# Second step of a forward 2-D transform: from fp32 matmuls to three fp16 passes over a split operand

## The chip, the cores and the metric

The kernel runs on one core of a Trainium2 chip. The metric is the device time of one execution in microseconds, the median of several runs. TensorE multiplies (its results land in PSUM), ScalarE and VectorE read PSUM and write SBUF, GpSimd is a third elementwise engine, and SyncE issues the DMAs. Each engine works through its own instructions in order, and the engines wait for each other through semaphores.

## The reference, cut to what matters

The input is `x` of shape (8, 128, 128, 128): 8 images, 128 channels, 128 x 128 pixels, fp32. The first of two layers takes the two-dimensional Fourier transform of every channel of the group-normalised image:

```
xf = jnp.fft.fft2(x)                       # x: b, c, h, w
qf = xf.reshape(b, HEADS, hd, h * w)       # frequency attention uses qf
g  = sigmoid(conv(relu(bn(conv(xf.real, w1)))))
out_f_l = jnp.abs(jnp.fft.ifft2(g * xf))
```

Everything after it (attention over heads, gates, inverse transform, spatial attention from 3x3 and 5x5 convolutions, and a second layer with a state-space scan) is left as it is by the change.

## The kernel before, in words

`layer0` does layer 0 in a hardware loop over the 8 images, `layer1` does layer 1 after it. Within an image the stages follow each other: load and group normalisation, **forward transform**, a Gram matrix over the spectrum, gates, inverse transform, head mixing, and the convolutions. This document is about the forward transform.

The forward transform of an image is done in `NK` = 32 steps of 4 channels (line 520). Step `t` has these parts, and each engine has them in its own program order:

- TensorE, `stage1(t)` (lines 1095 to 1100): 4 matmuls, each with one channel (128 x 128, fp32, from `xh`) as the stationary operand and the 128-column table `fwd` (65 cosine and 63 sine columns) as the moving one. They fill the PSUM bank `bk[t % 2]`.
- ScalarE, lines 1386 to 1389: one copy of 128 x 512 from that bank to `AB[:, t % 2]` in SBUF, two buffers in turn. Semaphore `s_ab` counts these copies.
- TensorE, `stage2(t)` (lines 1102 to 1111): 4 matmuls with a 128 x 128 cosine or sine table as the stationary operand and the 4 x 65 cosine part or the 4 x 63 sine part of `AB` as the moving one, two that accumulate in bank `bk[2 + t % 2]` (real part) and two in `bk[4 + t % 2]` (imaginary part). Each fp32 matmul shows as two records in the trace.
- ScalarE, `xr_copy(t)` (1380 to 1384) and VectorE, `xi_copy(t)` (712 to 716): each moves its part of the spectrum from PSUM to `XR`, `XI` (128 x 256) and `XLAST` (128 x 4) in SBUF.

The orders are these. TensorE: stage1(0), then for each t stage1(t+1), stage2(t). `stage1(t)` waits until the copy of step t-2 has left its bank; `stage2(t)` waits for the copy of step t and for both spectrum copies of step t-2. ScalarE: copy(t), xr_copy(t-1), and in steps 4, 12, 20 and 28 in addition `normalise` (1376 to 1378), which normalises a quarter of the image in place (128 x 4096). VectorE:

```
columns(0)
columns(1)
for i in range(8):
    for t in range(4 * i, 4 * i + 4):
        xi_copy(t)
    if i + 2 < 8:
        columns(i + 2)
```

`columns(i)` (718 to 722) normalises the 16 channels of group i in `xh` (two instructions over 128 x 2048), which the four `stage1` of that group read. `xh` has two buffers. The load of group i+2 is issued by SyncE (1008 to 1013) once `stage1(4i+3)`, the last reader of the buffer, is done: the kernel waits at line 1010 and then issues two DMAs of 8 channels.

Matmuls of all these stages are recorded under line 1066, ScalarE's operations under line 1365, since small helpers (`mm`, `cp`) issue them.

Of the kernel before, what the change touches and what calls it, by code (L numbers as in the profile page):

```python
# [27 lines left out]
F16 = mybir.dt.float16  # L28
ALU = mybir.AluOpType
# [12 lines left out]
NP = 6  # L42
T3W, T5W = 3 * NP, 5 * NP
VROWS = (0, 64, 1, 64, 64, 64, 64, 126, 64, 127)
XSCALE, WMAX = 32.0, 16384.0


# [82 lines left out]
def layer0(nc, B, x, table, shift_d, w, wts, y_d, of_d, x1, gn2):  # L130
# [3 lines left out]
    with ctx:  # L134
# [4 lines left out]
        def count(name, per):  # L139
            counters.append(Count(sem(name), per))  # L140
            return counters[-1]
# [51 lines left out]

        wk = lambda o, n: work[:, o:o + n]
        xh = wk(0, 4096).rearrange("p (s c w) -> p s c w", s=2, w=P)
        AB = wk(4096, 1024).rearrange("p (s c u) -> p s c u", s=2, u=P)
        T8 = wk(5120, 1024).rearrange("p (w j) -> p w j", j=JG)
        gates = wk(0, UG * P).rearrange("p (u c) -> p u c", c=P)
        Z = wk(2048, 2048).rearrange("p (s c n) -> p s c n", s=2, c=4)
# [173 lines left out]
        def _(dve):  # L373
# [8 lines left out]
            def link(op):  # L382
                s_ch[0] += 1
                op.then_inc(s_link, 1)
                dve.wait_ge(s_link, s_ch[0])
# [4 lines left out]
            for n, (name, _) in enumerate(plan):  # L390
                dve.wait_ge(s_ld, ld_at[n])
                if name == "first":
                    g = lambda i: par8[0:8, i:i + 1]
                    link(nc.vector.tensor_scalar(g(5), g(4), 1e-5, None, ALU.add))
                    dve.wait_ge(s_sq, 1)
                    link(nc.vector.reciprocal(g(5), g(5)))
                    link(nc.vector.tensor_tensor(g(6), g(1), g(5), ALU.mult))
                    link(nc.vector.tensor_tensor(g(7), g(0), g(3), ALU.subtract))
                    link(nc.vector.tensor_tensor(g(7), g(7), g(6), ALU.mult))
                    did(nc.vector.tensor_tensor(g(7), g(7), g(2), ALU.add))  # L400
                    dve.wait_ge(s_pe, next(npe))
                    nc.vector.tensor_copy(gate_sb[:, :], bk[0][0:UG * JG, 0:2])
                    nc.vector.tensor_copy(temps[:, :], bk[1][:, 0:2])
                    nc.vector.tensor_copy(w1t[:, :], bk[2][:, 0:8])
                    for i in range(4):
                        m = min(4, UG - 4 * i)
                        link(nc.vector.tensor_copy(gate_w[:, 4 * i:4 * i + m, :], bk[3 + i][0:UG * JG + 1, 0:m * P]))
                    link(nc.vector.tensor_copy(valid[:, :, :], ks["valid"].rearrange("t (r n) -> t r n", n=P)))
                    link(nc.vector.tensor_copy(vfix[:, :, :], ks["vfix"].rearrange("t (r n) -> t r n", n=P)))
                    link(nc.vector.memset(relu_r[:, :, :], 1.0))  # L410
                    did(nc.vector.memset(B8[:, :, :], 0.0))
                    nc.vector.memset(norms[:, 0, 0:1], 0.0).then_inc(s_go, 1)
                elif name.startswith("proj"):
                    dve.wait_ge(s_pe, next(npe))
                    s = int(name[4:])
                    link(nc.vector.tensor_copy(pt[:, 2 * s, :], bk[0][:, 0:P]))
                    did(nc.vector.tensor_copy(pt[:, 2 * s + 1, :], bk[1][:, 0:P]))
                    nc.vector.memset(norms[:, 0, 1:2], 0.0).then_inc(s_go, 1)
                elif name.startswith("qk"):
                    _, off, size = name.split()  # L420
                    off = int(off)
                    link(nc.vector.tensor_tensor(btap, ks["tap"].rearrange("p (t s) -> p t s", s=T5), bcol.unsqueeze(1).broadcast_to([P, T5, T5]), ALU.mult))
                    did(nc.vector.tensor_tensor(sparse, ks["mpair"].unsqueeze(1).broadcast_to([P, T5, 64]), w5.unsqueeze(2).broadcast_to([P, T5, 64]), ALU.mult))
                    dve.wait_ge(s_pe, next(npe))
                    dst = WBt if size == "5" else WAfull
                    for i in range(4):
                        m = min(8, T5 - 8 * i)
                        link(nc.vector.tensor_copy(dst[:, 8 * i:8 * i + m, off:off + 64], bk[i][:, 0:m * 64].rearrange("p (t o) -> p t o", o=64)))
                    did(nc.vector.tensor_copy(bias_sum[:, int(size == "5"), off:off + 64], bk[4][0:T5, 0:64]))
                    dve.wait_ge(s_ve, done[0])  # L430
                    nc.vector.memset(w5, 0.0).then_inc(s_go, 1)
                else:
                    s = int(name[3:])
                    for i in range(2):
                        dst = (WVt, WCt)[s].rearrange("p t (g i) -> p t g i", i=2)[:, :, :, i]
                        link(nc.vector.tensor_tensor(dst, ks["mgroup"].unsqueeze(1).broadcast_to([P, T5, 64]), w2[:, i, :].unsqueeze(2).broadcast_to([P, T5, 64]), ALU.mult))
                    if s == 0:
                        link(nc.vector.tensor_tensor(vtap[:, :, :], ks["vt"].rearrange("p (t s) -> p t s", s=T5), bcol.unsqueeze(1).broadcast_to([P, T5W, T5]), ALU.mult))
                    nc.vector.memset(w2, 0.0).then_inc(s_go, 1)
# [95 lines left out]
        s_xn = count("s_x_normalised", 4)  # L535
        s_xhn = count("s_columns_normalised", 8)
        s_s1 = count("s_stage1", NK)
        s_ab = count("s_stage1_copied", NK)
        s_s2 = count("s_stage2", NK)
        s_xr = count("s_real_copied", NK)  # L540
        s_xi = count("s_imag_copied", NK)
# [104 lines left out]

        @block.vector
        def _(dve):
            credit(dve, v, s_shi, s_xhn, s_xi, s_h1c, s_gx, vq, vf, s_pq, s_lq, s_pf, s_lf, s_ud, s_y, s_fd, s_ms, s_bvc, s_oa, s_x1, s_bn)
            V = nc.vector  # L650

            n0 = [0]
# [4 lines left out]
            with dve.Fori(0, B) as b:  # L657
# [54 lines left out]
                def xi_copy(t):  # L712
                    dve.wait_ge(s_s2.sem, s_s2.at(b, t + 1))
                    spectrum = bk[4 + t % 2][:, 0:4 * HALF].rearrange("p (c u) -> p c u", u=HALF)
                    V.tensor_copy(XLAST[:, 1, 4 * t:4 * t + 4], spectrum[:, :, U64])
                    V.tensor_copy(XI[:, 4 * t:4 * t + 4, :], spectrum[:, :, 0:U64]).then_inc(s_xi.sem, 1)

                def columns(i):
                    dve.wait_ge(sxh[i % 2], b * 128 + 32 * (i // 2) + 32)
# [2 lines left out]
                    V.tensor_tensor(t_, t_, rows[:, P + 16 * i:P + 16 * i + 16].unsqueeze(2).broadcast_to([P, 16, P]), ALU.add).then_inc(s_xhn.sem, 1)  # L722

                columns(0)
                columns(1)
                for i in range(8):
                    for t in range(4 * i, 4 * i + 4):
                        xi_copy(t)
                    if i + 2 < 8:
                        columns(i + 2)  # L730
# [333 lines left out]
        def _(pe):  # L1064
# [15 lines left out]
            with pe.Fori(0, B) as b:  # L1080
# [13 lines left out]

                def stage1(t):
                    pe.wait_ge(s_xhn.sem, s_xhn.at(b, t // 4 + 1))
                    pe.wait_ge(s_ab.sem, s_ab.at(b, t - 1))
                    for c in range(4):
                        m = mm(bk[t % 2][:, c * P:(c + 1) * P], xh[:, t // 4 % 2, 4 * (t % 4) + c, :], k["fwd"], start=True, stop=True)
                    m.then_inc(s_s1.sem, 1)  # L1100

                def stage2(t):
                    pe.wait_ge(s_ab.sem, s_ab.at(b, t + 1))
                    pe.wait_ge(s_xr.sem, s_xr.at(b, t - 1))
                    pe.wait_ge(s_xi.sem, s_xi.at(b, t - 1))
                    A, Bm = AB[:, t % 2, :, 0:HALF], AB[:, t % 2, :, HALF:]
                    for o, (ca, cb_) in ((bk[2 + t % 2], (k["cs"][:, 0:P], k["cs"][:, P:])), (bk[4 + t % 2], (k["sc"][:, 0:P], k["cs"][:, 0:P]))):
                        o3 = o[:, 0:4 * HALF].rearrange("p (c u) -> p c u", u=HALF)
                        mm(o3, ca, A, start=True, stop=False)
                        m = mm(o3[:, :, 1:64], cb_, Bm, start=False, stop=True)  # L1110
                    m.then_inc(s_s2.sem, 1)

                stage1(0)
# [249 lines left out]
        def _(act):  # L1363
            credit(act, a, s_row, s_hq, s_hf, s_last, s_sq, s_tt, s_trc, s_shr, s_xn, s_ab, s_xr, s_t8c, s_rel, s_sig, s_z, s_abs, s_uc, s_mc, s_os, s_of)
            cp = lambda o, i, f=ACT.Copy, **kw: nc.scalar.activation(o, i, f, **kw)  # L1365
            with act.Fori(0, B) as b:
# [13 lines left out]
                def xr_copy(t):  # L1380
                    act.wait_ge(s_s2.sem, s_s2.at(b, t + 1))
                    spectrum = bk[2 + t % 2][:, 0:4 * HALF].rearrange("p (c u) -> p c u", u=HALF)
                    cp(XLAST[:, 0, 4 * t:4 * t + 4], spectrum[:, :, U64])
                    cp(XR[:, 4 * t:4 * t + 4, :], spectrum[:, :, 0:U64]).then_inc(s_xr.sem, 1)

                for t in range(NK):
                    act.wait_ge(s_s1.sem, s_s1.at(b, t + 1))
                    act.wait_ge(s_s2.sem, s_s2.at(b, t - 1))
                    cp(AB[:, t % 2, :, :].rearrange("p c u -> p (c u)"), bk[t % 2][:, :]).then_inc(s_ab.sem, 1)
                    if t > 0:  # L1390
                        xr_copy(t - 1)
                    if t % 8 == 4:
                        normalise(t // 8)
# [839 lines left out]
```

## Time and profile before

| | us |
|---|---|
| median of 3 runs | 26842.19 |
| lowest and highest | 26841.0, 26844.8 |
| the profiled execution, its own time | 26840.82 |
| span of the profiled execution, first to last instruction | 26839.0 |
| TensorE busy in the span | 23909.5 |
| VectorE busy | 19661.7 |
| ScalarE busy | 13616.0 |
| GpSimd busy | 12340.1 |

Read the busy times as averages over stages that have different limits: about half of the span is layer 0 and half is layer 1. The forward transform of one image takes about 100 us of an image's 1,640 us in layer 0. Times in the rows are microseconds from the span's start, unless ns is written.

### The profile page before, as it was taken

What the parts mean: (1) busy time and instruction counts of PE and PEld (TensorE: products, weight loads), DVE (VectorE), ACT (ScalarE), POOL (GpSimd) and SP (SyncE); (2) the same over time, 40 slices, a digit from 0 to 9 for tenths busy, and PEclk for the clock granted to TensorE, in tenths of its full rate; (3) what the DMA queues carried; (4) which work ended last, traced back from release to release, by engine and by line L of the source; (5) the groups of instructions that cost most, each with busy time, mean ns of one, the idle gap of its engine ahead of it and who ended that gap; (6) DMA issues with size and microseconds to landing.
All of it is one profiled execution on the core that took longest, in us unless ns stands there. A gap on an engine that the chain in (4) does not pass through costs nothing. (4 is left out here: it accounts for less than half of the span.)

```text
span 26839.0 us, 328765 instructions
## 1 busy us (share of the span) xinstructions
PE 23909.5 (89%) x108001; PEld 14269.1 (53%) x108001; DVE 19661.7 (73%) x22753; ACT 13616.0 (51%) x19703; POOL 12340.1 (46%) x4613
## 2 busy tenths in 40 slices
PE   6988989889898998989988888888888888888888
PEld 4776867768677676877733333333333333333333
DVE  3562635537255372644699999999999999999999
ACT  1413223131321413214277777777777777777777
POOL 0000000000000000000099999999999999999998
PEclk7998989989898998989999999999999999999999
DMA  1121121211202112021244444444444444444444
GB/s 53 49 76 61 33 65 38 76 61 42 66 32 73 61 55 69 27 66 57 75 178 165 193 165 173 183 167 191 169 169 185 169 191 166 167 189 167 190 168 163
DMA packets 816277, 3112.23 MB, mean 116 GB/s; under 512 B 61865, under 2 KB 325434, under 8 KB 530362
## 3 DMA queue, kind: packets, MB, share of 16 engines
q1 hardware_dynamic: 815802, 3106.12, 31.1%
q8 instruction: 271, 4.44, 0.1%
q14 instruction: 204, 1.67, 0.0%
HBM read 2813.61 MB, written 292.30 MB: 116 GB/s over the span
## 5 line engine op out<-in xcount | busy, mean ns | idle before, releaser
L2176 POOL TENSOR_TENSOR hid<-hid,bc 128x2048 f32<-128x2048 f32 x2048 | 7814.6, 3816 | 909.2 <-DVE carry L2082 906.5
L1845 PE MATMUL yp<-hid,ident 128*128 128x512 f32 x16384 | 7344.7, 597 | 430.7 <-POOL hid L2176 430.7
L2150 POOL TENSOR_SCALAR_AFFINE_SELECT ident<-ident 128x128 f32<-128x128 f32 x1 | 0.3, 294 | 13331.3 <-DVE ident L2035 13331.3
L1845 PEld LDWEIGHTS yp<-hid,ident 128*128 128x128 f32 x16384 | 3039.7, 189 | 4628.3 <-issue 3957.9
L2068 DVE TENSOR_TENSOR_SCAN hid<-da,carry,t 128x512 f32<-128x512 f32 x3968 | 4857.8, 1266 | 111.0 <-DVE carry L2082 7.7
L2074 DVE TENSOR_TENSOR_SCAN hid<-t,carry,hid 128x512 f32<-128x512 f32 x3968 | 4828.1, 1258 | 29.2 <-ACT t L1916 28.5
L2169 POOL TENSOR_TENSOR hid<-bc,du 128x1024 f32<-128x1024 f32 x2048 | 4101.4, 2003 | 197.0 <-PE yp L1845 170.6
L1066 PE MATMUL bk<-region 128*128 128x256 f16 (+2 forms) x32688 | 3946.9, 279 | 24.6 <-ACT region L1365 19.1
L1066 PEld LDWEIGHTS bk<-region 128*128 128x128 f16 (+2 forms) x32688 | 3400.0, 119 | 603.9 <-issue 175.8
L1916 ACT ACTIVATE t<-delta,v_a 128x512 f32<-128x512 f32 x4096 | 2660.0, 681 | 1574.0 <-DVE hid L2074 1570.9
L1801 PE MATMUL pj<-xn,w_x 128*128 128x512 f32 x4096 | 2376.5, 734 | 1079.2 <-ACT xn L1941 1031.0
L1066 PE MATMUL bk<-work,region 128*128 128x256 f16 x27336 | 3151.6, 273 | 23.9 <-DVE region L960 20.3
L1066 PEld LDWEIGHTS bk<-work,region 128*128 128x128 f16 x27336 | 2643.9, 99 | 498.6 <-issue 74.5
L1927 ACT ACTIVATE t<-bc 128x1024 f32<-128x1024 f32 x2048 | 2096.6, 1024 | 1437.7 <-DVE hid L2068 1387.1
L1904 ACT ACTIVATE da<-delta,v_a 128x512 f32<-128x512 f32 x4096 | 2703.2, 707 | 0.3 <-DVE delta L2110 0.3
L2054 DVE TENSOR_TENSOR t<-t,du 128x1024 f32<-128x1024 f32 x2048 | 2479.0, 1210 | 256.4 <-ACT t L1927 256.2
L1365 ACT ACTIVATE work<-work 128x512 f32<-128x512 f32 (+3 forms) x656 | 696.4, 1062 | 3314.7 <-DVE work L865 1434.8
L1365 ACT ACTIVATE work<-bk 128x512 f32<-128x512 f32 (+1 forms) x1976 | 1094.3, 589 | 2331.3 <-PE bk L1066 2065.4
L1801 PEld LDWEIGHTS pj<-xn,w_x 128*128 128x128 f32 x4096 | 943.9, 237 | 2459.8 <-issue 2450.0
L846 DVE COPY work<-bk 128x512 f32<-128x512 f32 x640 | 442.7, 692 | 1897.5 <-PE bk L1066 1892.8
L1365 ACT ACTIVATE region<-work 128x512 f32 (+2 forms) x384 | 643.7, 1676 | 1789.3 <-DVE work L835 1569.3
L805 DVE COPY work<-bk 128x512 f32<-128x512 f32 x256 | 177.1, 692 | 1838.6 <-PE bk L1066 1838.6
(272 smaller groups left out, 24892.0 us busy)
## 6 DMA issues: line engine op xcount, KB each, us to landing
bc<-bc_rows SPq DMA_DIRECT2D x1024, 2048.0 KB, 7.2
work<-in_shift_d SPq DMA_DIRECT2D x256, 512.0 KB, 3.5
xpad<-in_x SPq DMA_DIRECT2D x32, 2048.0 KB, 18.8
work<-in_x SPq DMA_DIRECT2D x128, 512.0 KB, 4.8
gated<-work SPq DMA_DIRECT2D x256, 256.0 KB, 2.2
region<-gated SPq DMA_DIRECT2D x256, 256.0 KB, 2.9
region<-heads SPq DMA_DIRECT2D x256, 256.0 KB, 3.1
region<-in_x SPq DMA_DIRECT2D x256, 256.0 KB, 3.6
```

Source lines behind the costliest of these rows:

```text
L1066: mm = lambda *args, **kw: nc.tensor.matmul(*args, skip_group_check=True, **kw)
L1365: cp = lambda o, i, f=ACT.Copy, **kw: nc.scalar.activation(o, i, f, **kw)
L1801: m = nc.tensor.matmul(pj[h][:, :], w_x[:, t, h * P:(h + 1) * P], xn[:, t:t + CH], start=(t == 0), stop=(t == K4 - 1))
L1845: m = nc.tensor.matmul(yp[:, h, :], ident[:, :], hid[:, k % 4, n, :], start=False, stop=(g == G - 1 and n == 3), skip_group_check=True)
L1904: m = nc.scalar.activation(da[:, k % 2, j, :], delta[:, q, h, :], ACT.Exp, scale=v_a[:, h, 4 * g + j:4 * g + j + 1])
L1916: m = nc.scalar.activation(t1[:, j, :], delta[:, q, h, :], ACT.Exp, scale=v_a[:, h, 4 * g + 2 + j:4 * g + 3 + j])
L1927: nc.scalar.activation(t0[:, :, :], bc[:, g, 0, 0:2, :], ACT.Copy).then_inc(s_t0.sem, 1)
L2054: nc.vector.tensor_tensor(t0[:, :, :], t0[:, :, :], du[:, q, h, :].unsqueeze(1).broadcast_to([P, 2, CH]), ALU.mult).then_inc(s_m.sem, 1)
L2068: m = nc.vector.tensor_tensor_scan(hid[:, k % 4, j, :], da[:, k % 2, j, :], t0[:, j, :], first(j), ALU.mult, ALU.add)
L2074: m = nc.vector.tensor_tensor_scan(o, t1[:, j - 2, :], o, first(j), ALU.mult, ALU.add)
L2169: nc.gpsimd.tensor_tensor(hid[:, k % 4, 2:4, :], bc[:, g, 0, 2:4, :], du[:, q, h, :].unsqueeze(1).broadcast_to([P, 2, CH]), ALU.mult).then ...
L2176: nc.gpsimd.tensor_tensor(hid[:, k % 4, :, :], hid[:, k % 4, :, :], bc[:, g, 1, :, :], ALU.mult).then_inc(s_hc.sem, 1)
```

## The change

Stage 2 is done on fp16 operands. The result of stage 1, times 16, is written as a high half (the value rounded to fp16) and a low half (what is left, in fp16), and the cosine and sine tables, times 16384, are held in the same way in a new tile `dft`. A product is then three fp16 matmuls: high table with high data, high table with low data, low table with high data. ScalarE writes the high half where it made the fp32 copy before. VectorE writes the low half in a new function `ab_low`, which waits for stage 1 of the step and for the high half. Both stages of TensorE that waited for `s_ab` now wait for the low half's semaphore `s_abl`. The two spectrum copies divide by 16 x 16384 as they copy. Four instructions in the set-up at the start of the kernel fill `dft`. The four banks, the two `AB` buffers and their place in `work` are the same ones.

```diff
+ASCALE, CSCALE = 16.0, 16384.0
...
-        AB = wk(4096, 1024).rearrange("p (s c u) -> p s c u", s=2, u=P)
+        AB = wk(4096, 1024).bitcast(F16).rearrange("p (s h c u) -> p s h c u", s=2, h=2, u=P)
+        ab_flat = wk(4096, 1024).bitcast(F16).rearrange("p (s h n) -> p s h n", s=2, h=2)
+        dft = sb("dft16", [P, 2, 3 * P], F16)
...
+                    for i, part in enumerate((k["cs"], k["sc"][:, 0:P])):
+                        of_i = slice(2 * P * i, 2 * P * i + (2 - i) * P)
+                        link(nc.vector.tensor_scalar(dft[:, 0, of_i], part, CSCALE, None, ALU.mult))
+                        link(nc.vector.scalar_tensor_tensor(dft[:, 1, of_i], part, CSCALE, dft[:, 0, of_i], ALU.mult, ALU.subtract))
...
VectorE:
-                    V.tensor_copy(XLAST[:, 1, 4 * t:4 * t + 4], spectrum[:, :, U64])
-                    V.tensor_copy(XI[:, 4 * t:4 * t + 4, :], spectrum[:, :, 0:U64]).then_inc(s_xi.sem, 1)
+                    back_by = 1.0 / (ASCALE * CSCALE)
+                    V.tensor_scalar(XLAST[:, 1, 4 * t:4 * t + 4], spectrum[:, :, U64], back_by, None, ALU.mult)
+                    V.tensor_scalar(XI[:, 4 * t:4 * t + 4, :], spectrum[:, :, 0:U64], back_by, None, ALU.mult).then_inc(s_xi.sem, 1)
+
+                def ab_low(t):
+                    dve.wait_ge(s_s1.sem, s_s1.at(b, t + 1))
+                    dve.wait_ge(s_ab.sem, s_ab.at(b, t + 1))
+                    V.scalar_tensor_tensor(ab_flat[:, t % 2, 1], bk[t % 2][:, :], ASCALE, ab_flat[:, t % 2, 0], ALU.mult, ALU.subtract).then_inc(s_abl.sem, 1)
...
                 columns(0)
+                ab_low(0)
                 columns(1)
                 for i in range(8):
                     for t in range(4 * i, 4 * i + 4):
+                        if t + 1 < NK:
+                            ab_low(t + 1)
                         xi_copy(t)
                     if i + 2 < 8:
                         columns(i + 2)
...
TensorE, stage1:
-                    pe.wait_ge(s_ab.sem, s_ab.at(b, t - 1))
+                    pe.wait_ge(s_abl.sem, s_abl.at(b, t - 1))
...
TensorE, stage2:
-                    pe.wait_ge(s_ab.sem, s_ab.at(b, t + 1))
+                    pe.wait_ge(s_abl.sem, s_abl.at(b, t + 1))
...
-                        mm(o3, ca, A, start=True, stop=False)
-                        m = mm(o3[:, :, 1:64], cb_, Bm, start=False, stop=True)
+                        for wh, ph in ((0, 0), (0, 1), (1, 0)):
+                            mm(o3, dft[:, wh, ca:ca + P], AB[:, t % 2, ph, :, 0:HALF], start=(wh == 0 and ph == 0), stop=False)
+                        for wh, ph in ((0, 0), (0, 1), (1, 0)):
+                            m = mm(o3[:, :, 1:64], dft[:, wh, cb_:cb_ + P], AB[:, t % 2, ph, :, HALF:], start=False, stop=(wh == 1))
...
ScalarE:
-                    cp(AB[:, t % 2, :, :].rearrange("p c u -> p (c u)"), bk[t % 2][:, :]).then_inc(s_ab.sem, 1)
+                    cp(ab_flat[:, t % 2, 0], bk[t % 2][:, :], scale=ASCALE).then_inc(s_ab.sem, 1)
```

## Rows read from the trace of the kernel before

**Rows 1.** The page, section 1: busy time, share of the span, instructions.

```profile
PE 23909.5 (89%) x108001; PEld 14269.1 (53%) x108001; DVE 19661.7 (73%) x22753; ACT 13616.0 (51%) x19703; POOL 12340.1 (46%) x4613
```

**Rows 2.** Busy time by stretch: the first image's forward transform.

```profile
core 0: us, PE busy (x) PEld busy (x) DVE busy (x) ACT busy (x) POOL busy (x), PEclk, DMA share, GB/s
...
257.00:357.00 100.00, 88.49 (x514) 79.89 (x515) 51.97 (x81) 47.01 (x100) 0.00 (x0) 0.95 0.22 64
```

**Rows 3.** Groups of instructions by line and shape, 257 to 357 us.

```profile
L1066 PE MATMUL bk<-work,ctab 128*128 128x260 f32 x128 | 39.6, 390 | 5.6 <-ACT work L1365 4.9 <-DVE region L716 0.5
...
L721 DVE TENSOR_TENSOR work<-work 128x2048 f32<-128x2048 f32 x8 | 18.3, 2292 | 3.6 <-DMA work<-in_x 3.5
...
L1365 ACT ACTIVATE xpad<-xpad,small 128x4096 f32<-128x4096 f32 x4 | 15.3, 3833 | 0.0
```

**Rows 4.** Timeline, steps 2 to 4 of the first image (start, duration, engine).

```profile
271.66 0.60 ACT L1365 ACTIVATE work<-bk 128x512 f32<-128x512 f32 x1 [0.44 <-PE bk L1066]
271.79 1.00 SPq L1013 DMA_DIRECT2D work<-in_x  x2
...
274.08 1.89 PE L1066 MATMUL bk<-work,ctab 128*128 128x260 f32 x8
274.28 0.60 ACT L1365 ACTIVATE work<-bk 128x512 f32<-128x512 f32 x1 [0.44 <-PE bk L1066]
...
275.81 1.05 PE L1066 MATMUL bk<-ctab,work 128*128 128x128 f32 x8
...
276.01 0.16 DVE L715 COPY region<-bk 128x4 f32<-128x4 f32 x1 [2.12 <-PE bk L1066]
276.09 0.41 DVE L716 COPY region<-bk 128x256 f32<-128x256 f32 x1
276.35 3.83 ACT L1365 ACTIVATE xpad<-xpad,small 128x4096 f32<-128x4096 f32 x1
...
277.15 2.29 DVE L721 TENSOR_TENSOR work<-work 128x2048 f32<-128x2048 f32 x1 [0.65 <-DMA work<-in_x]
```

**Rows 5.** Timeline, the first image's beginning, groups of four, and end.

```profile
257.53 2.29 DVE L721 TENSOR_TENSOR work<-work 128x2048 f32<-128x2048 f32 x1
```

```profile
283.64 0.60 ACT L1365 ACTIVATE work<-bk 128x512 f32<-128x512 f32 x1 [0.44 <-PE bk L1066]
```

```profile
306.46 0.60 ACT L1365 ACTIVATE work<-bk 128x512 f32<-128x512 f32 x1 [0.44 <-PE bk L1066]
```

```profile
355.88 0.41 DVE L716 COPY region<-bk 128x256 f32<-128x256 f32 x1
```

**Rows 6.** Line 721 over the run: min, median, max ns, first and last start.

```profile
L721 DVE TENSOR_TENSOR work<-work x64: 2283/2293/2294, 257.5 to 11813.6; 128x2048 f32<-128x2048 f32 x64
```

**Rows 7.** Timeline, a convolution stage: fp16 weight loads that pace 256-column matmuls.

```profile
1003.79 2.29 PEld L1066 LDWEIGHTS bk<-region 128*128 128x128 f16 x21
```

**Rows 8.** Groups of VectorE instructions by line and shape, whole run.

```profile
L841 DVE SCALAR_TENSOR_TENSOR work<-work 128x3168 f16<-128x3168 f32 x128 | 441.4, 3448 | 25.4 <-ACT work L1365 23.8 <-DVE work L934 1.5
...
L849 DVE TENSOR_TENSOR work<-bk,work 128x512 f32<-128x512 f32 x640 | 435.5, 681 | 0.0
L980 DVE SCALAR_TENSOR_TENSOR region<-work,small,region 128x512 f32<-128x512 f32 x256 | 192.5, 752 | 63.4 <-DVE work L973 47.4
```

**Rows 9.** Busy time by stretch around TensorE's gaps (columns as in rows 2).

```profile
1457.10:1459.70 2.60, 0.07 (x2) 0.03 (x2) 2.31 (x8) 0.00 (x0) 0.00 (x0) 1.00 0.00 0
1459.70:1466.40 6.70, 6.70 (x60) 5.66 (x60) 6.53 (x10) 0.00 (x0) 0.00 (x0) 1.00 0.01 2
...
3098.30:3100.90 2.60, 0.07 (x2) 0.02 (x2) 2.31 (x8) 0.00 (x0) 0.00 (x0) 0.76 0.00 0
3100.90:3106.50 5.60, 5.60 (x27) 3.94 (x28) 5.46 (x9) 0.00 (x0) 0.00 (x0) 0.50 0.00 0
...
3797.20:3802.00 4.80, 0.05 (x2) 0.04 (x1) 2.99 (x3) 1.75 (x4) 0.00 (x0) 0.73 0.00 0
3802.00:3809.00 7.00, 5.12 (x8) 2.19 (x8) 5.92 (x2) 1.04 (x3) 0.00 (x0) 0.70 0.00 0
```

More of the change, by code:

```diff
@@ L537, in layer0 @@
         s_s1 = count("s_stage1", NK)
-        s_ab = count("s_stage1_copied", NK)
+        s_ab = count("s_stage1_high", NK)
+        s_abl = count("s_stage1_low", NK)
         s_s2 = count("s_stage2", NK)
@@ L648, in _ @@
         def _(dve):
-            credit(dve, v, s_shi, s_xhn, s_xi, s_h1c, s_gx, vq, vf, s_pq, s_lq, s_pf, s_lf, s_ud, s_y, s_fd, s_ms, s_bvc, s_oa, s_x1, s_bn)
+            credit(dve, v, s_abl, s_shi, s_xhn, s_xi, s_h1c, s_gx, vq, vf, s_pq, s_lq, s_pf, s_lf, s_ud, s_y, s_fd, s_ms, s_bvc, s_oa, s_x1, s_bn)
             V = nc.vector
@@ L1102, in stage2 @@
                 def stage2(t):
-                    pe.wait_ge(s_ab.sem, s_ab.at(b, t + 1))
+                    pe.wait_ge(s_abl.sem, s_abl.at(b, t + 1))
                     pe.wait_ge(s_xr.sem, s_xr.at(b, t - 1))
                     pe.wait_ge(s_xi.sem, s_xi.at(b, t - 1))
-                    A, Bm = AB[:, t % 2, :, 0:HALF], AB[:, t % 2, :, HALF:]
-                    for o, (ca, cb_) in ((bk[2 + t % 2], (k["cs"][:, 0:P], k["cs"][:, P:])), (bk[4 + t % 2], (k["sc"][:, 0:P], k["cs"][:, 0:P]))):
+                    COS, NSIN, SIN = 0, P, 2 * P
+                    for o, (ca, cb_) in ((bk[2 + t % 2], (COS, NSIN)), (bk[4 + t % 2], (SIN, COS))):
                         o3 = o[:, 0:4 * HALF].rearrange("p (c u) -> p c u", u=HALF)
-                        mm(o3, ca, A, start=True, stop=False)
-                        m = mm(o3[:, :, 1:64], cb_, Bm, start=False, stop=True)
+                        for wh, ph in ((0, 0), (0, 1), (1, 0)):
+                            mm(o3, dft[:, wh, ca:ca + P], AB[:, t % 2, ph, :, 0:HALF], start=(wh == 0 and ph == 0), stop=False)
+                        for wh, ph in ((0, 0), (0, 1), (1, 0)):
+                            m = mm(o3[:, :, 1:64], dft[:, wh, cb_:cb_ + P], AB[:, t % 2, ph, :, HALF:], start=False, stop=(wh == 1))
                     m.then_inc(s_s2.sem, 1)
@@ L1382, in xr_copy @@
                     spectrum = bk[2 + t % 2][:, 0:4 * HALF].rearrange("p (c u) -> p c u", u=HALF)
-                    cp(XLAST[:, 0, 4 * t:4 * t + 4], spectrum[:, :, U64])
-                    cp(XR[:, 4 * t:4 * t + 4, :], spectrum[:, :, 0:U64]).then_inc(s_xr.sem, 1)
+                    back_by = 1.0 / (ASCALE * CSCALE)
+                    cp(XLAST[:, 0, 4 * t:4 * t + 4], spectrum[:, :, U64], scale=back_by)
+                    cp(XR[:, 4 * t:4 * t + 4, :], spectrum[:, :, 0:U64], scale=back_by).then_inc(s_xr.sem, 1)
                 for t in range(NK):
```

## The prediction

> **What bounds the kernel now.** I read the page first: TensorE is busy for 89% of the span [rows 1], but that is an average over stages, so the stage that the diff touches has to be read by itself. The view by stretches gives it for the first image: in 100 us TensorE is busy for 88.5, VectorE for 52, ScalarE for 47 [rows 2]. TensorE sets the pace there, and both readers of PSUM look half free. The groups by shape say how it is filled and what it waits for: 5.6 us of gaps ahead of stage 2, nearly all for ScalarE's copy [rows 3]. The timeline then gives the rhythm. The ScalarE copies of two undisturbed steps start at 271.66 and 274.28, so a step takes 2.62 us; stage 2 starts at 274.08 and the next stage 1 at 275.81, so stage 2 takes 1.73 us and stage 1 the other 0.89. VectorE sees stage 2's result at 276.01, 0.20 after the next stage could start [rows 4]. In four steps that is 10.5 us, yet 283.64 to 306.46 holds two groups of four: 11.4 us for one [rows 5]. The missing 0.9 us is mostly the 3.8 us normalisation on ScalarE, every second group.
>
> The row to see before costing anything is `columns`. Its first instruction starts at 277.15 and had waited 0.65 us for its load, which was issued at 271.79, when stage 1 of step 3 had been seen done at 271.66 [rows 4]. So a load lands 5.49 us after that stage, and `columns` then holds VectorE for 2 x 2.29 = 4.58 us [rows 3]. Today nothing urgent is queued behind it: the two `xi_copy` that it delays are needed only two steps later.
>
> **The parts of the change.**
>
> *TensorE, stage 2.* Eight fp32 records (1.73 us) go, twelve fp16 matmuls of 260 or 252 columns come. In the convolutions 21 fp16 weight loads, one for each 256-column matmul, take 2.29 us, 0.109 us each [rows 7]. So the new stage 2 takes 12 x 0.109 = 1.31 us, 0.42 less. Over 256 steps that is 108 us, if TensorE went on setting the pace. The nearest rows from the other side are the same matmuls at half clock, 27 in 5.6 us, 0.207 each [rows 9], which gives 2.5 us; it is the upper bound if the 65-element rows of fp16 data stream badly. I take 0.109, because the convolutions too read short shifted rows of fp16. The Trainium skill (TensorE: Matmul & The Clock Gate, Back-to-back issue gap) has about 81 ns for 128 and 131 ns for 512 columns in a stream of loads and matmuls; an estimate between them is 98 ns at 256, and stage 2 would take 1.17 us by it. The row is 11% above it, and the row is used.
>
> *ScalarE.* The high half is the old copy with a scale and a narrower output: 0.60 us as before [rows 4]. I cost it and the scale in both spectrum copies at nothing, since element counts and sources stay; what hides an error is ScalarE's idle half, and without that cover 0.1 us on each copy would be 0.1 us a step.
>
> *VectorE.* `xi_copy` stays at 0.49 us (0.16 and 0.41, which start 0.08 apart [rows 4]). `ab_low` is new: 128 x 512, one source in PSUM, two tensors in, fp16 out. Rows for one such size are 0.681 (tensor-tensor from PSUM) and 0.752 (scalar-tensor-tensor in SBUF); the fp16-writing form on 3168 elements takes 3.448, or 0.56 for 512 by proportion [rows 8]. Bounds 0.56 and 0.80; I take 0.72, between the two full-size ones. VectorE then has 4 x (0.72 + 0.49) + 4.58 = 9.4 us of work in four steps, where TensorE has 4 x 2.2 = 8.8. VectorE is just the fuller engine even with perfect overlap, but the order matters more.
>
> *The wait.* `ab_low(t+1)` stands in VectorE's queue ahead of `xi_copy(t)`, and `ab_low` of a group's second step stands behind `columns`. Both stages of TensorE now wait for it. Take 0 where stage 1 of step 4i+3 is seen done. The load of `columns(i+2)` lands at 5.49, `columns` runs to 10.07, `ab_low(4i+5)` to 10.79, stage 2 of that step starts 0.05 later and takes 1.31, stage 1 of step 4i+7 takes 0.89 and is seen 0.20 after that:
>
> 5.49 + 4.58 + 0.72 + 0.05 + 1.31 + 0.89 + 0.20 = **13.24 us for four steps**, against 11.41 now.
>
> Only one of the four stage 2 is on this chain, so 0.42 us of the saving counts and the rest is idle time. Ahead of it TensorE has stage 2 of 4i+2 to 4i+4 and stage 1 of 4i+4 to 4i+6, for which every low half is there in time. They end at 3 x (1.31 + 0.89) - 0.20 = 6.4, and then there is nothing until 10.84: **a gap of 4.4 us**, six times an image. ScalarE's normalisation lies inside it.
>
> *The ends of the stage.* At the start `ab_low(0)` stands ahead of `columns(1)`: `columns(0)` 4.58, stage 1 at half clock 1.7 (8 x 0.213, twice 0.107), seen 0.2 later, high 0.60, low 0.72 with its waits 0.1, `columns(1)` 4.58, low 0.72, stage 2 1.31, stage 1 0.89, seen 0.20: 15.6 us to the end of step 3's stage 1, where the trace has 271.66 - 257.53 = 14.1 [rows 4, 5]. The last group has no `columns` but a normalisation: 2.2 to step 28's stage 1, high 0.6 and xr_copy to 1.76, normalisation 3.83, high 0.60, low 0.77, then 1.31 + 0.89 + 0.20 + 0.05 = 11.6. The tail, two stages 2 and the last copies behind the last stage 1, is 3.4.
>
> Sum: 15.6 + 6 x 13.24 + 11.6 + 3.4 = 110.0 us an image. Now it is 257.53 to 356.29 = 98.8 [rows 5]. **+11.2 us an image, +90 us for 8** (the first image stands for all: line 721 has 64 instructions, 8 an image, alike within 1% [rows 6]).
>
> *TensorE's clock.* The rows show what a gap among dense matmuls does. At 1457 a gap of 2.6 us left the clock full. At 3098 the same gap brought it to half level (1.2 of 2.4 GHz), and the whole 5.6 us behind it ran at half: 2.8 us lost. At 3797 a gap of 4.8 us had a granted clock of 0.73 in it and 0.70 in the 7 us behind it, so 2.6 and 4.2 us of half level: 2.1 us lost where matmuls wanted it [rows 9]. The new gap, 4.4 us, is nearly that last one, followed by 4.4 us of dense work that all stands on the chain. I take 2.0 us for each of 6 gaps, 12 us an image, **+96 us in all**; the bounds are 0 and 7 gaps x 2.8, or 157 us (the seventh is ScalarE's normalisation in the last group). The Trainium skill (TensorE: Matmul & The Clock Gate, HAM oscillation) speaks against the change in the same way: a loop whose bursts are parted by idle waits starts each burst at half rate again. The rows agree for the longer gaps and say "sometimes" for the short one.
>
> *Set-up.* Four linked VectorE instructions over 768 columns in all at the start, 1.1 us by the proportion of the 0.752 us for 512 [rows 8]: about +1 us, once, on the path. No DMA, and nothing on GpSimd or SyncE, is added. SyncE waits for stage 1 before it issues the column loads, so they shift with it. `stage1`'s wait for `s_abl` instead of `s_ab` is hidden, since stage 2 ahead of it needs a later low half only one step on.
>
> Against the profiled execution, 26840.8 us: + 90 + 96 + 1 = 27028. The median of the runs lies 1.4 us above that execution: 27029 us.
>
> **The rivals.** About 0.2% (54 us) is what a measurement of this kernel can tell from no change.
>
> *A: the gaps are there and the clock holds.* For it: the gap at 1457. Against: every gap over 4 us in the rows has half level behind it. Time: 26842 + 91 = 26933.
>
> *B: TensorE keeps the pace, the kernel gets faster.* The mechanism is that `columns` does not keep the low half from stage 2, because its load lands early and VectorE is through before TensorE runs dry. The place is line 721's wait. The point that decides is 11.4 us for four steps: landing plus `columns` plus `ab_low` would have to shrink from 10.8 to under 9.0. With all of it hidden the time is 26842 - 108 = 26734. For it: VectorE's half-empty average. Against: the 0.65 us wait for the load and 4.6 us of `columns`, neither of which the change touches.
>
> *C: the passes are not cheap.* The change gives fp16 matmuls but not at 0.109 us, with 65 and 63 elements between jumps and odd start addresses. At 0.207 stage 2 takes 2.5 us and TensorE has 3.4 us a step, 13.5 in a group, and the chain above becomes 14.4 us with its longer stage 2, with shorter gaps and less of a clock loss. That is some 25 to 35 us an image: 27040 to 27120. Against: convolutions read shifted fp16 rows at full rate.
>
> *D: the two nearly cancel* (loads that land a microsecond earlier, no clock loss): 26842 + 8 x (11.2 - 7 x 1) = about 26876.
>
> **How the numbers follow.** The forecast has 0.70, A 0.12, C 0.08, B 0.05, D 0.05. The forecast's own spread is 26985 to 27085 (the clock at 1 to 2.8 us a gap and `ab_low` at 0.56 to 0.80, which is 1 us an image down or 0.5 up). The range reaches down to A and up to the clock's upper bound: 26915 to 27090. It leaves out B, D, most of C and the forecast's edges, 2 in 10. Faster by over 0.2%: 0.05 (B). Within 0.2%: 0.06 (D and a little of A). Slower: 0.89.
>
> **What the profile will show.** Right: in the forward transform TensorE gaps of about 4.4 us that end in VectorE's low half, six an image; VectorE's `columns` waiting for the load for 0.5 to 1.5 us; ScalarE copies of steps 4i+3 about 13.2 us apart at full clock and 15 with the clock's loss; a granted clock well under 1.0 in this stage; twelve fp16 matmuls in 1.3 us; an image's stage at 118 to 124 us. A stage that stays under 99 us proves the chain wrong; one near 109 with a clock of 1.0 is A; fp16 matmuls 0.2 us apart at full clock are C.

## The result, and the profile after

The changed kernel takes 27048.25 us (median of 4 runs, 27036.2 to 27064.7), the kernel before 26843.49 us beside it: a ratio of 1.0077, 95% interval 1.0064 to 1.009. That is 205 us slower. The forecast was 27029 us, in a range of 26915 to 27090.

The busy time by stretch shows the forward transform of the first image. Its columns are those of [rows 2], which it answers to.

```profile
core 0: us, PE busy (x) PEld busy (x) DVE busy (x) ACT busy (x) POOL busy (x), PEclk, DMA share, GB/s
260.10:382.70 122.60, 88.02 (x640) 75.88 (x640) 71.75 (x112) 47.01 (x100) 0.00 (x0) 0.84 0.18 52
...
297.30:301.40 4.10, 0.02 (x1) 0.00 (x0) 4.07 (x5) 0.60 (x1) 0.00 (x0) 0.84 0.00 0
301.40:306.90 5.50, 5.46 (x26) 4.36 (x27) 1.73 (x6) 1.04 (x3) 0.00 (x0) 0.50 0.00 0
306.90:311.90 5.00, 5.00 (x47) 4.56 (x46) 2.06 (x6) 2.89 (x6) 0.00 (x0) 1.00 0.72 211
```

The stage has gone from 98.8 us [rows 5] to 122.6, TensorE is idle for 34.6 us of it, and the granted clock has come down to 0.84. The last three lines are one of the gaps: 4.1 us with no matmul, 5.5 us at half clock with 26 matmuls, then 47 matmuls in 5.0 us at full clock. The waits of the same stretch name what ends the gaps:

```profile
PEld bk L1083 <- DVE work L730: 31.3, 10, 4.5
PE bk L1083 <- DVE work L730: 29.2, 8, 4.3
DVE work L730 <- ACT work L1384: 27.3, 17, 4.3
...
DVE work L735 <- DMA work<-in_x: 8.3, 6, 1.6
```

Line 730 is `ab_low`. TensorE waits 29.2 us for it, where before the change 0.5 us of its waits ahead of stage 2 were on VectorE [rows 3]. The groups by shape, as in [rows 3], give the prices:

```profile
L1083 PEld LDWEIGHTS bk<-work,dft 128*128 128x128 f16 x384 | 41.0, 109 | 40.5 <-DVE work L730 31.3
...
L730 DVE SCALAR_TENSOR_TENSOR work<-bk,work 128x512 f16<-128x512 f32 x32 | 22.0, 687 | 27.3 <-ACT work L1384 27.3
L1384 ACT ACTIVATE work<-bk 128x512 f16<-128x512 f32 x32 | 19.2, 600 | 24.4 <-PE bk L1083 24.4
```

The timeline shows one group of four with its chain, and answers to [rows 4, 5]:

```profile
290.65 0.60 ACT L1384 ACTIVATE work<-bk 128x512 f16<-128x512 f32 x1 [0.66 <-PE bk L1083]
...
292.58 1.33 PEld L1083 LDWEIGHTS bk<-work,dft 128*128 128x128 f16 x12
...
296.17 2.29 DVE L735 TENSOR_TENSOR work<-work 128x2048 f32<-128x2048 f32 x1 [1.44 <-DMA work<-in_x]
...
298.49 2.29 DVE L736 TENSOR_TENSOR work<-work 128x2048 f32<-128x2048 f32 x1
300.70 0.68 DVE L730 SCALAR_TENSOR_TENSOR work<-bk,work 128x512 f16<-128x512 f32 x1
...
301.44 2.76 PE L1083 MATMUL bk<-work,dft 128*128 128x260 f16 x12 [4.12 <-DVE work L730]
...
303.99 1.91 PE L1083 MATMUL bk<-ctab,work 128*128 128x128 f32 x8
...
305.94 0.60 ACT L1384 ACTIVATE work<-bk 128x512 f16<-128x512 f32 x1 [1.26 <-PE bk L1083]
```

Stage 1 of the group's last step is seen done at 290.65. Then come the load (5.52 us), the two column instructions (4.6), the low half, and at 301.44 stage 2, after a gap of 4.12 us. The twelve fp16 matmuls of stage 2 take 2.55 us until the next stage 1 starts (303.99), where they take 1.34 at full clock. The end of the next group is seen at 305.94. That is 15.3 us for the group, where the kernel before needs 11.4.

In the two traces the stage, from the first column instruction to the end of the last imaginary copy, is 98.9 us before and 122.4 after, mean of 8 images (121.99 to 122.66). That is 188 us of the 207.5 by which the span grew. The first image's stage starts 2.6 us later, layer 1 took 10 us longer (13508 and 13518 us), and the rest of layer 0 about 7 us. The 10 us are not tied to this stage: in the traces of all eight other kernels below, layer 1 took 3 to 10 us longer than in the trace of before.

### The profile page after: what moved, and what is told of

Its sections match the earlier page's. It is cut to its first block and busy times, and to the rows that moved or that the text cites. A ratio compares the mean times of both kernels' runs of the same rounds, so it can differ in the third digit from the quotient of the medians.

```text
span 27046.5 us, 331330 instructions
## 1 busy us (share of the span) xinstructions
PE 23910.8 (88%) x109025; PEld 14238.7 (53%) x109025; DVE 19825.9 (73%) x23013; ACT 13616.5 (50%) x19703; POOL 12339.9 (46%) x4613
## 5 line engine op out<-in xcount | busy, mean ns | idle before, releaser
L1083 PE MATMUL bk<-work,region 128*128 128x256 f16 x27336 | 3158.8, 273 | 23.9 <-DVE region L977 20.3
L1384 ACT ACTIVATE work<-bk 128x512 f32<-128x512 f32 (+2 forms) x1976 | 1094.2, 589 | 2359.0 <-PE bk L1083 2093.1
```

The lines of the kernel that those rows point to most:

```text
L1083: mm = lambda *args, **kw: nc.tensor.matmul(*args, skip_group_check=True, **kw)
```

## The experiments

Eight more kernels were run, each beside the kernel before on the same chip. The median of the kernel before was between 26842.6 and 26846.3 us each time; the table gives the one measured beside the changed kernel (26843.5). "Stage" is the mean over 8 images of the time from the first column instruction to the end of the last imaginary copy, and "half clock" the mean time in it at the lower clock (1.2 of 2.4 GHz).

| run | us | ratio to before, 95% | stage, us | half clock in it, us |
|---|---|---|---|---|
| before | 26843 | | 98.9 | 9.3 |
| changed | 27048 | 1.0077 (1.0064 to 1.0090) | 122.4 | 39.8 |
| e1_wait_only | 27027 | 1.0068 (1.0051 to 1.0084) | 120.5 | 20.3 |
| e4_filler | 26982 | 1.0049 (1.0032 to 1.0065) | 112.4 | 9.1 |
| e2_quarters | 26831 | 0.9995 (0.9985 to 1.0005) | 97.2 | 15.0 |
| e3_before_quarters | 26834 | 0.9996 (0.9987 to 1.0005) | 94.2 | 5.8 |
| e7_pool_columns | 26786 | 0.9977 (0.9967 to 0.9987) | 89.4 | 11.0 |
| e8_before_pool_columns | 26816 | 0.9990 (0.9981 to 0.9999) | 95.4 | 7.0 |
| e9_pool_split | 26689 | 0.9943 (0.9929 to 0.9956) | 77.4 | 6.8 |
| e10_before_pool_split | 26781 | 0.9977 (0.9968 to 0.9986) | 89.2 | 6.6 |

**e1_wait_only: the new wait without the fp16 passes.** The kernel before, plus the low half, which nothing reads.

```diff
+                def ab_low(t):
+                    dve.wait_ge(s_s1.sem, s_s1.at(b, t + 1))
+                    dve.wait_ge(s_ab.sem, s_ab.at(b, t + 1))
+                    V.scalar_tensor_tensor(low_flat[:, t % 2], bk[t % 2][:, :], 16.0, AB[:, t % 2, :, :].rearrange("p c u -> p (c u)"), ALU.mult, ALU.subtract).then_inc(s_abl.sem, 1)
...
-                    pe.wait_ge(s_ab.sem, s_ab.at(b, t + 1))
+                    pe.wait_ge(s_abl.sem, s_abl.at(b, t + 1))
```

> The kernel before, with its fp32 second step, plus the low half alone: VectorE computes it into a spare buffer that nothing reads, and both stages of TensorE wait for it. My theory (the wait behind the column normalisation is the cost): four steps take 5.49 + 4.58 + 0.69 + 0.05 + 1.73 + 0.89 + 0.20 = 13.6 us at full clock, TensorE's gap shrinks from 4.1 to about 3 us so that the clock falls less often, and an image's forward transform takes 114 to 117 us: 26960 to 26990 us. Rival (the fp16 passes, their clock or their operands cost the time): near the kernel before, 99 to 101 us an image, 26840 to 26860 us.

It took 27027 us, 181 us more than the kernel before in the same session (26846), where the whole change costs 205. So the wait alone costs most of it, and the rival is out. The expectation of 26960 to 26990 us was missed by 37 us. The timeline has the group at full clock where it was put (290.04 to 303.71, 13.67 us):

```profile
290.04 0.60 ACT L1375 ACTIVATE work<-bk 128x512 f32<-128x512 f32 x1 [0.44 <-PE bk L1076]
...
300.79 1.99 PE L1076 MATMUL bk<-work,ctab 128*128 128x260 f32 x8 [2.92 <-DVE work L723]
...
303.71 0.60 ACT L1375 ACTIVATE work<-bk 128x512 f32<-128x512 f32 x1 [0.44 <-PE bk L1076]
```

What was mis-sized is the clock. The busy times of the second and the fourth image:

```profile
1918.80:2041.30 122.50, 95.86 (x512) 85.04 (x512) 72.30 (x112) 47.01 (x100) 0.00 (x0) 0.89 0.18 52
5243.90:5359.40 115.50, 88.21 (x512) 79.09 (x512) 72.23 (x112) 47.01 (x100) 0.00 (x0) 0.96 0.19 55
```

The fourth image, with gaps of 2.9 to 3.2 us, keeps the full clock (0.96 includes the cold start) and takes 115.5 us, as expected; the second loses it and takes 122.5. In the second a load that landed 0.5 us late made the first of these gaps 3.5 us long. But a late load is not needed. Two gaps of the seventh image, both with loads on time (5.5 us), each with the 5 us behind it:

```profile
10254.00:10256.90 2.90, 0.00 (x0) 0.00 (x0) 2.90 (x4) 1.99 (x5) 0.00 (x0) 0.94 0.01 3
10256.90:10261.90 5.00, 4.99 (x20) 4.31 (x21) 1.44 (x5) 1.04 (x3) 0.00 (x0) 0.70 0.00 0
10269.10:10272.10 3.00, 0.05 (x2) 0.02 (x1) 2.97 (x4) 0.60 (x1) 0.00 (x0) 1.00 0.00 0
10272.10:10277.10 5.00, 5.00 (x30) 4.56 (x31) 2.47 (x7) 1.41 (x5) 0.00 (x0) 1.00 0.10 23
```

The first gap was followed by a clock of 0.70, the second by 1.00.

The fp16 passes on top of this wait did not help: the changed kernel is 21 us slower than e1 (0.08%, from two sessions; the runs of the two do not overlap), and by the traces 16 of them are in this stage. They make the bursts shorter and the gaps longer (3.3 to 4.5 us), and the half-clock time doubles from 20 to 40 us.

**e4_filler: the gaps filled with useless matmuls.**

```diff
+                    for _ in range({5: 20, 9: 20, 13: 20, 17: 20, 21: 20, 25: 20, 29: 10}.get(t, 0)):
+                        mm(bk[7][:, 0:3 * P], dft[:, 0, 0:P], dft[:, 0, :], start=True, stop=True)
                     stage2(t)
```

> The changed kernel, with 20 extra fp16 matmuls of 384 columns (3.2 us) into an unused bank in each of TensorE's six gaps of an image, and 10 in the gap of the last group. They add work and take away nothing. My theory (a good half of the loss is the clock that falls in the gap): the clock stays full from the second group on, an image takes 110 to 113 us in place of 122.4, 26940 to 26965 us. Rival (the clock is no part of it, or falls for another reason): 122 us an image or more, 27048 us or more.

130 more matmuls an image, and the kernel is 66 us faster than the changed one. The stage is 112.4 us:

```profile
259.10:371.90 112.80, 96.63 (x770) 79.73 (x770) 71.53 (x112) 47.03 (x100) 0.00 (x0) 0.96 0.19 57
```

The timeline of one group has the same chain, now at full clock. The filler starts at 323.70, stage 2 starts at 327.98 behind the low half, and takes 1.51 us where the changed kernel's took 2.76:

```profile
323.70 3.41 PE L1083 MATMUL bk<-dft 128*128 128x384 f16 x20
...
327.25 0.68 DVE L730 SCALAR_TENSOR_TENSOR work<-bk,work 128x512 f16<-128x512 f32 x1
...
327.98 1.51 PE L1083 MATMUL bk<-work,dft 128*128 128x260 f16 x12 [0.87 <-DVE work L730]
```

So of the 23.5 us an image, 10.0 are the clock and 13.5 the chain. The split is known to about 1 us: e4's six loads of an image landed 1.3 us later in sum than those of the changed kernel, and with loads alike the clock's share would be 11.3 and the chain's 12.2. The whole was expected at 26940 to 26965 and came out 17 us above it. The stage itself is as expected; the rest of an image took 3 us longer than in the changed kernel in this trace (1544.9 against 1541.8 us), which stays unexplained.

**e2_quarters: the column work cut, so that nothing stands behind 4.6 us.** `columns(q)` now does 4 channels; five of them run ahead, then one after each `xi_copy`.

```diff
+                for q in range(5):
+                    columns(q)
+                ab_low(0)
+                for t in range(NK):
+                    if t + 1 < NK:
+                        ab_low(t + 1)
+                    xi_copy(t)
+                    if t + 5 < NK:
+                        columns(t + 5)
```

> The changed kernel with the column normalisation on VectorE cut into quarters of 4 channels, one after each imaginary copy, so that a low half waits behind 1.2 us and not 4.6. My theory: the gaps go; VectorE is the bound with 0.69 + 0.49 + 1.25 = 2.4 us a step, 32 steps and a start make 93 to 99 us an image: 26800 to 26845 us, about the kernel before. Rival (the longer chain stage 1, high, low, stage 2 costs the time wherever the columns stand): over 105 us an image, over 26890 us.

The same arithmetic as the changed kernel in another order: 217 us less. The rival is out, since the chain stage 1, high, low, stage 2 is still there. The stage is 97.2 us. In the first image TensorE still waits 14.9 us for the low half, and VectorE is busy for 77%:

```profile
260.80:358.60 97.80, 80.81 (x640) 70.85 (x640) 75.18 (x160) 47.02 (x100) 0.00 (x0) 0.92 0.22 66
```

The larger part of that wait is not VectorE's load of work. Four gaps of 2.3 to 2.4 us end in a low half whose high half had stood behind one of the four image normalisations on ScalarE (steps 4, 12, 20 and 28):

```profile
299.27 3.83 ACT L1384 ACTIVATE xpad<-xpad,small 128x4096 f32<-128x4096 f32 x1
...
303.00 0.60 ACT L1384 ACTIVATE work<-bk 128x512 f16<-128x512 f32 x1
...
303.69 0.69 DVE L730 SCALAR_TENSOR_TENSOR work<-bk,work 128x512 f16<-128x512 f32 x1 [1.55 <-ACT work L1384]
...
304.44 2.76 PE L1083 MATMUL bk<-work,dft 128*128 128x260 f16 x12 [2.33 <-DVE work L730]
```

**e3_before_quarters: the same cut in the kernel before.**

> The kernel before (fp32 second step), with only its column normalisation cut into quarters on VectorE, as e2 has it. It says how much of e2 comes from the cut alone. My theory: nothing urgent stands behind the columns in the kernel before, so the cut gives only the earlier start and a little of the stalls: 93 to 97 us an image, 26800 to 26830 us. Rival (the cut helps the fp32 kernel as much as the fp16 one, 25 us an image): under 80 us an image, 26690 us.

It is not told from the kernel before in total (26834 us, interval 0.9987 to 1.0005). The stage became 4.7 us shorter, 38 us in all by the traces, of which the whole shows 9. Most of it came back in stages that the cut does not touch: the rest of layer 0 took 20 us longer than in the trace of before, layer 1 took 10. Such stretches differ from kernel to kernel in these traces (1007.0 to 1010.2 us an image, mean of 7, from VectorE's first 128x3168 instruction of the convolutions to the next image's first column instruction), and no run says why.

**e7_pool_columns: the column work on GpSimd, in quarters.** The loop over q stands in GpSimd's program, with a semaphore for the row of factors; VectorE keeps `ab_low` and `xi_copy`.

```diff
+            with pool.Fori(0, B) as b:
+                pool.wait_ge(s_rw.sem, s_rw.at(b, 1))
+                for q in range(32):
...
+                    pool.wait_ge(sxh[i % 2], b * 128 + 32 * (i // 2) + 32)
+                    G.tensor_tensor(t_, t_, rows[:, 4 * q:4 * q + 4].unsqueeze(2).broadcast_to([P, 4, P]), ALU.mult).then_inc(s_c1.sem, 1)
...
+                    G.tensor_tensor(t_, t_, rows[:, P + 4 * q:P + 4 * q + 4].unsqueeze(2).broadcast_to([P, 4, P]), ALU.add).then_inc(s_xhn.sem, 1)
```

> The changed kernel with the column normalisation on GpSimd, in quarters of 4 channels; VectorE keeps the low halves and the imaginary copies. From GpSimd's rows (128x2048 in 3.8 us, 128x1024 in 2.0) a quarter takes 2 x 1.0 us, just under TensorE's 2.2 us a step. My theory: TensorE sets the pace at 2.2 us a step with a full clock, 76 to 84 us an image, 26660 to 26730 us. Rival (GpSimd is the new bound, because it is slower on these shapes or while VectorE works): 2.4 to 3 us a step, 85 to 100 us an image, 26730 to 26850 us.

The fp16 kernel is now faster than the kernel before (0.9977), but the stage is 89.4 us and not 76 to 84, and the time lies above the expected 26660 to 26730 us. Both numbers are those of the rival, which named GpSimd as the cause; the cause is another. A quarter takes GpSimd 2 x 1.04 us, less than a step of 2.23, and TensorE's gaps end elsewhere:

```profile
294.13 3.83 ACT L1376 ACTIVATE xpad<-xpad,small 128x4096 f32<-128x4096 f32 x1
...
297.85 0.59 ACT L1376 ACTIVATE work<-bk 128x512 f16<-128x512 f32 x1
...
298.55 0.69 DVE L732 SCALAR_TENSOR_TENSOR work<-bk,work 128x512 f16<-128x512 f32 x1 [4.26 <-ACT work L1376]
...
299.30 0.40 PE L1075 MATMUL bk<-work,dft 128*128 128x260 f16 x2 [2.41 <-DVE work L732]
```

VectorE waited 4.26 us for the high half, which stood behind the image normalisation in ScalarE's queue. In the changed kernel that lay inside a longer gap, as the prediction had it; with that gap gone it is what is late next, as in e2. e9 below tests this.

**e8_before_pool_columns: the same move in the kernel before.**

> The kernel before (fp32 second step) with its column normalisation on GpSimd in quarters, as e7 has it. My theory: VectorE was not its bound; the four normalisations on ScalarE (3.83 us each) still stop TensorE for 1.2 us each; 92 to 97 us an image, 26790 to 26830 us. Then e7, at 89.4 us an image, is ahead of it by the fp16 passes, by less than 0.42 x 32 = 13 us, because ScalarE's normalisation costs e7 2.4 us four times. Rival: GpSimd's column work slows TensorE's operands or the loads: 98 us or more.

26816 us, and 95.4 us a stage: the rival is out, and the fp16 passes are 6 us an image ahead in this arrangement.

**e9_pool_split and e10_before_pool_split: both cuts, with fp16 and with fp32.** The image normalisation goes in 32 pieces of 4 rows, one in each step.

```diff
-                    part = xpad[:, 2 + 32 * i:34 + 32 * i, 2:2 + P]
+                    part = xpad[:, 2 + 4 * i:6 + 4 * i, 2:2 + P]
...
-                    if t % 8 == 4:
-                        normalise(t // 8)
+                    normalise(t)
```

> e7 (fp16 passes, columns on GpSimd), and the image normalisation on ScalarE cut from four pieces of 128x4096 into 32 of 128x512, one in each step after the real copy. e7 had four TensorE gaps of 2.4 us an image, which ended in a low half whose high half had stood behind such a piece. My theory: the last gaps go, TensorE sets the pace with 2.23 us a step at full clock, 76 to 80 us an image: 26680 to 26720 us. Rival (GpSimd's 2.08 us for a quarter and its loads are the next bound): 84 us or more, 26740 us or more.

> The kernel before (fp32 second step) with both cuts of e9: columns on GpSimd in quarters, image normalisation in 32 pieces. Beside e9 it says what the fp16 passes are worth where no other engine holds TensorE up. My theory: 2.62 us a step, 88 to 91 us an image, 26765 to 26800 us, so the fp16 passes save 10 to 13 us an image, 80 to 105 us in all. Rival (the fp16 passes save nothing in themselves): as e9, within 20 us.

Both came out inside their expectations. e9 beats both kernels: 26689 us, 0.9943 of before (0.9929 to 0.9956), 359 us faster than the changed kernel with the same matmuls. Its first image, and then e10's:

```profile
259.20:336.00 76.80, 73.64 (x640) 67.17 (x640) 35.00 (x96) 52.62 (x128) 65.29 (x64) 0.96 0.29 83
```

```profile
257.50:346.20 88.70, 85.84 (x512) 78.26 (x512) 15.78 (x64) 52.57 (x128) 65.36 (x64) 0.97 0.24 72
```

TensorE is busy for 96% of e9's stage. Two steps of its timeline start stage 2 at 300.85 and 303.08, 2.23 us apart, against 2.62 before:

```profile
300.85 1.50 PE L1075 MATMUL bk<-work,dft 128*128 128x260 f16 x12
...
303.08 1.50 PE L1075 MATMUL bk<-work,dft 128*128 128x260 f16 x12
```

The fp16 passes are worth 89.2 - 77.4 = 11.8 us an image here, 94 us in all, and the two medians differ by 92.

## Why the prediction was right

*The promise.* Stage 2 was put at 1.31 us from the convolutions' rows and takes 1.33. The estimate from the figures of the Trainium skill (TensorE: Matmul & The Clock Gate, Back-to-back issue gap), 1.17, was too low. That the saving would be 108 us if TensorE set the pace holds to within 16 us, as e9 and e10 show. Rival C is out: with 65 and 63 fp16 elements between jumps the matmuls follow each other at 0.11 us, as the convolutions' do.

*The chain.* 13.24 us for a group of four at full clock. In the changed kernel no group behind a gap has a full clock, so the sum is read from e4: groups whose load landed on time were 13.1 to 13.3 us apart. Its terms: load 5.49, measured 5.52 in the group shown; columns 4.58, measured 4.53 from first start to `ab_low`; low half 0.72, measured 0.69; from there to the copy of the group's last step 2.45, measured 2.50; gap 4.4, measured 4.1. e1 confirms the chain by itself, with 13.67 us against 13.6 expected, and e2 and e7 by its removal. One term was taken too evenly: the load. In e4 some loads landed 6 to 7.4 us after the stage that frees their buffer, and such groups took 14 to 15 us. In sum that is 2.1 us an image, the larger part of the difference between 112.4 us and the 110.0 of the sum. No run moved the load alone off the chain, so its share is read from the timeline.

*The clock.* 12 us an image were forecast, 10.0 measured (122.4 less e4's 112.4), or 11.3 with e4's late loads allowed for. The chain says 10.5: from the end of the low half behind `columns` to ScalarE's copy of the group's last step it is 4.25 us in the changed kernel, mean of 48 groups, and 2.50 in e4. The chosen row, the gap of 4.8 us, was right in kind. Behind each of the 48 gaps of 3.3 to 4.5 us the clock was at half level for 2.7 to 6.0 us, 4.4 on average, where the row had 4.2. Rival A is out by this, while in e1 gaps of 2.9 us went either way.

One reason given for the 2.0 us a gap was wrong. The prediction had all the dense work behind a gap on the chain. Only one stage 2 and one stage 1 are on it, 2.2 us at full clock. In the group shown, half clock lasts 5.5 us behind the gap, but the chain loses 2.1 us: 4.50 from 301.44 to 305.94, where 2.40 was the sum. That is the most that any of the 48 groups lost, so the upper bound of 2.8 us a gap was too high.

The Trainium skill (TensorE: Matmul & The Clock Gate, HAM oscillation) describes bursts that all start at half rate behind waits of about 3 to 5 us. The changed kernel's gaps of 3.3 to 4.5 us agree with it: half clock came behind each of them. e1's gaps of 2.9 us are just shorter than the waits that it describes.

*The sum.* 23.2 us an image were forecast (11.2 and 12), 23.5 measured. That it is so near is partly luck: the chain was put 1 to 2 us too low and the clock 1 to 2 us too high. The set-up was put at 1 us. The stage starts 2.6 us later, but in e1, which has no tables to fill, it starts 2.4 us later, so this is no measure of them.

*What was costed at nothing.* The scale and the fp16 output on ScalarE: 0.60 us as before. The scale in the imaginary copies: 0.41 us as before. ScalarE's normalisation was put inside the gap, with no price of its own; e7 shows what it costs when that cover goes: 89.4 - 77.4 = 12 us an image.

*What the prediction did not see.* It counted the shorter stage 2 as a gain of 0.42 us a group. Each group does gain that on its chain, but against e1 the kernel lost 21 us in all: a shorter burst in front of a fixed wait leaves a longer gap, and the clock costs the chain 10.5 us an image here and 4.6 in e1. And 17 us of the span's 207 lie outside the stage and the start. They were not forecast, they are most of the 19 us between forecast and result, and they are of the size by which the untouched stages differ between kernels here.

## What to carry to other kernels

Before an operation joins the chain of the engine that sets the pace, look for the longest single instruction that can stand ahead of it in its engine's queue, and at the load that this one waits for. Busy shares do not show it: VectorE was half idle, and the chain still went from 11.4 to 13.2 us. Cut such work into pieces of a step's size, or give it to an engine that nobody waits for, first; then the cheaper matmuls pay. When TensorE's work shrinks but its wait does not, count the clock too.

## What the runs showed of the hardware

Useless matmuls can pay: e4's filler took the half-clock time of a stage from 39.8 to 9.1 us. Whether a gap of 2.9 us between the same bursts costs the clock differs within one image of one execution: one such gap in e1 was followed by a granted clock of 0.70, the next by 1.00. GpSimd worked for 65 of 77 us on the same SBUF buffer that TensorE read from, with no cost that shows: in e9 VectorE's low half takes 0.69 us as before and a step 2.23 us. VectorE's instructions beside it all read PSUM; none that reads two SBUF operands ran there.
